# Window attention beside a recurrence: scores in row packs, turned early, with the output divided in the turned layout

## What is computed

```python
def step(yt, wx_t):                      # L2_ffn: t = t + ys
    yt = jax.nn.sigmoid(wx_t + yt @ Vt)
    return (yt, yt)
...
def _window_attn(q, k, v, pos):          # L3_conv: x = x + out, x normed over channels first
    ...
    sim = jnp.einsum('bnhid,bnhjd->bnhij', qh * SCALE, kh) + pos
    attn = jax.nn.softmax(sim, axis=-1)
    out = jnp.einsum('bnhij,bnhjd->bnhid', attn, vh)
    return out.transpose(0, 1, 3, 2, 4).reshape(B, n, m, c)
...
# four quarters of 8 channels, 2 heads of 4: within windows of 8x8 (q1) and 16x16 (q3),
# across windows of 8x8 (q2) and 16x16 (q4)
out = jnp.concatenate([out_1, out_2], axis=-1)
return out @ Wo + bo
```

## Time and profile before

| | |
|---|---|
| median of 3 runs | 1141.13 us (1139.81 to 1141.36) |
| profiled execution, its own time | 1142.24 us |
| its span | 1140.40 us |
| recurrence, first 521 steps | 459.6 to 726.6 |
| the other steps | 726.6 to 1016.8 |
| second half's norm and projections | 1016.8 to 1044.1 |
| the attention's ring and mixing | 1044.1 to 1108.0 |
| experts, output | 1108.0 to the end |

### The profile page before, as it was taken

How to read it: one execution, slowest core, us unless ns; L and a number is a source line. 1 busy time by engine, 2 the same in 40 slices (tenths; PEclk the granted TensorE clock), 3 DMA queues, 4 the chain that set the end, 5 groups by cost and what they waited for, 6 DMA issues and landing times. The chain is left out here.

```text
span 1140.4 us, 12008 instructions
## 1 busy us (share of the span) xinstructions
PE 769.6 (67%) x4425; PEld 447.3 (39%) x4425; DVE 453.1 (40%) x785; ACT 473.4 (42%) x1595; POOL 261.6 (23%) x147
## 2 busy tenths in 40 slices
PE   7917878888768787455555555468985555568986
PEld 3302333333334343333333333346763333335753
DVE  5597999999766546000000000111120000028653
ACT  4446767776436422333333333322223333345542
POOL 3277989898600000300000000000000000002200
PEclk9957999999995687555555555555555555557997
DMA  2020000000000001000000000000000000000000
GB/s 65 2 55 0 1 0 1 1 0 1 1 5 1 1 21 47 24 1 1 0 1 1 1 1 1 1 1 1 1 1 1 0 1 1 1 1 1 1 14 17
DMA packets 9571, 7.70 MB, mean 7 GB/s; under 512 B 7154, under 2 KB 8066, under 8 KB 9224
## 3 DMA queue, kind: packets, MB, share of 16 engines
q1 hardware_dynamic: 9512, 6.93, 2.5%
HBM read 5.09 MB, written 0.26 MB: 5 GB/s over the span
## 5 line engine op out<-in xcount | busy, mean ns | idle before, releaser
L852 PE MATMUL L2p_z<-L2yx,L2v 64*32 64x2 f32 x2048 | 268.6, 199 | 240.3 <-ACT L2yx L862 235.3
L862 ACT ACTIVATE L2yx<-L2p_z 32x2 f32<-32x2 f32 x1024 | 165.0, 161 | 389.3 <-PE L2p_z L852 389.3
L852 PEld LDWEIGHTS L2p_z<-L2yx,L2v 64*32 64x32 f32 x2048 | 180.7, 136 | 337.8 <-ACT L2yx L862 315.5
L750 DVE COPY xn<-L2yx 32x512 f32<-32x512 f32 x2 | 0.8, 417 | 430.9 <-ACT L2yx L862 264.1
L629 POOL TENSOR_TENSOR hc<-hs,cb 128x1024 f32<-128x1024 f32 x64 | 149.4, 2355 | 20.6 <-DVE hs L612 20.5
L1588 POOL COPY xo<-xn 64x256 f32<-64x256 f32 (+1 forms) x6 | 4.0, 692 | 555.4 <-DVE xn L165 555.4
L556 PE MATMUL p_y<-hc,ident 128*128 128x512 f32 x256 | 122.8, 602 | 5.0 <-DVE y_seq L595 2.8
L612 DVE TENSOR_TENSOR_SCAN hs<-d_a,p_bb 128x1024 f32<-128x1024 f32 x48 | 109.8, 2286 | 7.3 <-ACT d_a L579 1.1
L583 ACT ACTIVATE cb<-p_cb 128x1024 f32<-128x1024 f32 x64 | 65.0, 1016 | 7.0 <-PE p_cb L546 6.7
L556 PEld LDWEIGHTS p_y<-hc,ident 128*128 128x128 f32 x256 | 47.7, 191 | 50.0 <-issue 31.5
L579 ACT ACTIVATE d_a<-step,decay 128x1016 f32<-128x1016 f32 x48 | 54.6, 1138 | 23.8 <-DVE hs L612 23.2
(11 more groups left out here) (427 smaller groups left out, 981.1 us busy)
## 6 DMA issues: line engine op xcount, KB each, us to landing
y_seq<-in_pick SPq DMA_DIRECT2D x1, 768.0 KB
b_parts<-part SPq DMA_DIRECT2D x3, 256.0 KB, 3.7
c_parts<-part SPq DMA_DIRECT2D x3, 256.0 KB, 4.5
pos<-in_pos SPq DMA_DIRECT2D x1, 512.0 KB, 3.6
ao<-in_at_o SPq DMA_DIRECT2D x1, 512.0 KB, 4.0
L1w<-in_L_w SPq DMA_DIRECT2D x1, 297.0 KB
L3w<-in_L_w SPq DMA_DIRECT2D x1, 297.0 KB
x_tok<-in_x SPq DMA_DIRECT2D x2, 128.0 KB, 3.0
```

What stands on the lines that cost most here:

```text
L852: pe.matmul(p_z[0:C, t % 2, 0:NB], v[:, 0:C], yx[:, NB * t:NB * (t + 1)], start=True, stop=True).then_inc(s("preact"), 1)
L862: act.activation(yx[0:C, NB * (t + 1):NB * (t + 2)], p_z[0:C, t % 2, 0:NB], ACT.Sigmoid).then_inc(s("state"), 1)
```

## The change

`Front` is made once and works on three *parts*: tiles 0 to 3, tiles 4 to 6, tile 7 (`PARTS`). The first two run beside the recurrence, from steps 517 and 901 on, the last in one block behind it (`rest`), which also holds the whole ring. The norm takes its inverse root on VectorE, by an integer start and three refinements, and has no step on ScalarE. `q` is one tensor; a score reads the 32 rows of its `j`, and the four `j` of a unit stand in four PSUM banks. A unit is now one tile (or two for the 8x8 windows) with all four `j`. For 7 of 12 units scores are made beside the recurrence, the row maximum is subtracted there on VectorE (`shifted`), and the result is turned and copied (`turn_scores`, `copy_turned`); the exponential comes afterwards, on turned scores, over 1024 columns at once, without a sum. Unused columns of the values are ones, so the product with the values gives the sum too, and the output is turned, divided (`divide`) and turned back. Biases and queries carry the other sign, so that VectorE's accumulated minimum is the negated maximum.

The core of the diff:

```diff
-                    HALF, ROOTS = T // 2, T // 2 + 24
-                    first = beside(s2)
+                    HALF, BULK = T // 2, T - 128
+                    front = beside(s2, by_batch)
...
-                            others = first.pe(pe)
+                            others = front.pe(pe)
...
+                                if t == BULK + 5:
+                                    others = itertools.chain(others, front.pe_bulk(pe))
                                 if t > HALF + 4:
                                     next(others, None)
...
-                                if t == ROOTS:
-                                    first.roots(act)
...
-                            add_half(dve, by_batch, 0)
-                            first.dve(dve)
+                            front.add_states(dve, 0)
+                            front.dve(dve)
+                            dve.wait_ge(s("state"), BULK)
+                            front.add_states(dve, 1)
+                            front.dve_bulk(dve)
...
-                            first.pool(pool)
-                    second = beside(s2)
-                    with nc.Block() as block:
...
-                            add_half(dve, by_batch, 1)
-                            second.dve(dve)
...
+                            front.pool(pool)
+                    front.rest(p_z)
...
-        q = sb("q", [128, 2, NB * HEADS, T], stack=st)
...
+        q = sb("q", [128, 2, T], stack=st)
...
-        NU, EARLY = len(units), len(units) // 2
...
+        units = [(2, 0), (2, 1), (2, 2), (2, 3), (0, 0), (0, 2), (0, 4), (0, 6), (2, 4), (2, 5), (2, 6), (2, 7)]
+        NU, FIRST, EARLY = len(units), 6, 7
+        BY_ACT = (8, 10)
...
-                last = dve.tensor_tensor_reduce(scored[:, i % EARLY, c], src[:, c], bias, 1.0, -3e38, ALU.add, ALU.max, mx[:, i, e:e + 1])
...
-                last = act.activation(row, row, ACT.Exp, bias=nmx[:, i, e:e + 1], accum_out=den[:, i, e:e + 1])
...
-                last = dve.tensor_scalar(row, row, rden[:, i, e:e + 1], None, ALU.mult)
...
+            rows = slice(32 * j, 32 * j + 32)
+            if g == 2:
...
+                return pe.matmul(dst[:, 0:KEYS], q[rows, 0, t * 128:(t + 1) * 128], kk[rows, 0, k0:k0 + KEYS], start=True, stop=True)
...
+                ins = dve.tensor_tensor_reduce(scored[:, u % EARLY, j, c], banks[j][:, c], bias, 1.0, 3e38, ALU.add, ALU.min, nmx[:, u, j, n:n + 1])
...
+            dve.tensor_tensor(row, row, least, ALU.subtract).then_inc(sig["at_shifted"], 1)
...
+            PARTS = ((0, 4), (4, 7), (7, 8))
+            ORDER = ((2, 0), (2, 0), (0, 2))
...
+                for _ in range(3):
+                    link(dve.tensor_tensor(step, root, root, ALU.mult))
+                    link(dve.tensor_tensor(step, step, half_var, ALU.mult))
+                    link(dve.scalar_tensor_tensor(root, step, 1.5, root, ALU.add, ALU.mult))
+                dve.tensor_tensor(tok, tok, spread(root), ALU.mult).then_inc(sig["part_scaled"], 1)
...
+            def turn_scores(self, pe, u):
+
+                pe.wait_ge(sig["at_shifted"], u + 1)
+                for n in range(2):
+                    s = 2 * u + n
+                    if s >= 2:
+                        pe.wait_ge(sig["weights_in"], s - 1)
+                    for j in range(NJ):
+                        last = pe.transpose(self.turn_banks[n][:, j * 128:(j + 1) * 128], scored[:, u, j, n * 128:(n + 1) * 128], ident[:])
+                        if j == NJ - 1:
+                            last.then_inc(sig["scores_turned"], 1)
+                        yield
...
+            def score_early(self, pe, u):
+                for n in range(1 if units[u][0] == 2 else 2):
+                    for j in range(NJ):
+                        ins = score(pe, self.early_banks[j], u, j, n)
+                        if units[u][0] == 2 or n == 1:
+                            ins.then_inc(sig["at_scores"], 1)
+                    yield
...
+                for u in range(FIRST):
+                    if u:
+                        pe.wait_ge(sig["at_max"], NJ * u)
+                    yield from self.score_early(pe, u)
+                    if u:
+                        yield from self.turn_scores(pe, u - 1)
+                    for _ in range(4 if u else 9):
...
+            def pe_bulk(self, pe):
+
+                p_q = self.p_q
+                pe.wait_ge(sig["weights_in"], 2 * FIRST)
+                yield from self.turn(pe, 1)
+                for _ in range(12):
+                    yield
+                yield from self.turn_back(pe, 1)
+                for _ in range(4):
+                    yield
+                pe.wait_ge(sig["at_max"], NJ * FIRST)
+                made = 4
+                for k, g in enumerate((2, 0)):
+                    pe.wait_ge(sig["xo_made"], 2 + k + 1)
+                    for m, wgt in enumerate((aq, ak)):
+                        if made >= 6:
+                            pe.wait_ge(sig["qk_read"], made - 1)
+                        self.project(pe, 1, g, wgt, p_q[:, m])
+                        made += 1
+                        for _ in range(3):
+                            yield
+                yield from self.pieces(pe, 0, *self.half_pieces())
+                for _ in range(6):
+                    yield
+                pe.wait_ge(sig["qk_read"], 8)
+                pe.wait_ge(sig["e_read"], 2)
+                yield from self.score_early(pe, FIRST)
+                for _ in range(9):
+                    yield
+                yield from self.turn_scores(pe, FIRST)
+
...
+                dve.wait_ge(sig["e_made"], 2)
+                self.copy_pieces(dve, 0, *self.half_pieces())
+                biased(dve, self.early_banks, FIRST)
+                shifted(dve, FIRST)
+                self.copy_turned(dve, FIRST)
...
+                RING = ["o0", "o1", "b0", "s14", "s15", "b1", "s16", "s17", "o2", "s18", "s19", "b2", "s20", "s21", "s22", "s23",
+                        "out", "o3", "b3"]
...
+                            kt, to = (t // 2 * 2 + n, t) if g == 2 else (t + n, t + n)
+                            for j in range(NJ):
+                                last = pe.matmul(p_o[32 * j:32 * j + 32, to % 4 * 128:(to % 4 + 1) * 128], vv[:, WITHIN[g], kt, j],
+                                                 weights[:, u % EARLY, n, j * 128:(j + 1) * 128], start=(g == 0 or n == 0), stop=(g == 0 or n == 1))
...
+                        def late_scores(u):
+                            for j, n in [(j, n) for j in range(NJ) for n in range(1 if units[u][0] == 2 else 2)]:
+                                if n == 0 and u > EARLY:
+                                    pe.wait_ge(sig["at_max"], NJ * (u - 1) + j + 1)
+                                ins = score(pe, late_banks[j], u, j, n)
+                                if units[u][0] == 2 or n == 1:
+                                    ins.then_inc(sig["at_scores"], 1)
...
+                        keep_streaming(pe, p_o, 2)
+                        for _ in self.turn(pe, 2):
+                            pass
+                        keep_streaming(pe, p_o, 3)
+                        for s in range(6):
+                            values(s)
+                        for _ in self.turn_back(pe, 2):
+                            pass
+                        values(6)
+                        values(7)
+                        for n, (wgt, g) in enumerate(((aq, 0), (ak, 0), (aq, 2), (ak, 2))):
+                            pe.wait_ge(sig["xo_made"], 4 + n // 2 + 1)
+                            self.project(pe, 2, g, wgt, p_q[:, n // 2, n % 2 * 128:(n % 2 + 1) * 128])
+                        for _ in self.pieces(pe, 1, *self.half_pieces()):
+                            pass
+                        for s in range(8, 10):
+                            values(s)
+                        pe.wait_ge(sig["qk_read"], 12)
+                        late_scores(7)
...
+                        values(23)
+                        turn_out()
+                        turn_run(3)
+                        mix_across()
+                        turn_run_back(3)
+                        mix_run(3)
...
+                            link(dve.reciprocal(over, src[:, :, :, HC:HC + 1]))
+                            dve.tensor_tensor(o_norm[:, i % 2, :, 0:16].rearrange("p t (j c) -> p t j c", c=HC), src[:, :, :, 0:HC],
+                                              over.broadcast_to([128, 4, NJ, HC]), ALU.mult).then_inc(read_sem(f"o{i}"), 1)
+
+                        self.add_states(dve, 2)
+                        self.norm(dve, link, 2)
+                        for n, g in enumerate((0, 2)):
+                            dve.wait_ge(sig["qk_made"], 8 + 2 * n + 2)
+                            self.copy_queries(dve, 2, g, p_q[:, n, 0:128])
+                            self.copy_keys(dve, 2, g, p_q[:, n, 128:256])
+                        dve.wait_ge(sig["e_made"], 3)
```

(29 more changed lines are left out.)

900 lines of the change are left out of this document (493 added, 407 removed).

## The result

Over four executions the changed kernel took 1098.77 us in the median (1096.21 to 1100.04), the kernel before 1140.6 on the same chip: a ratio of 0.962 with an interval of 0.960 to 0.964. The forecast was 1102, with a range of 1092 to 1124. The execution that was profiled is the shortest of the four: 1096.21 us, span 1094.3.

What follows compares the result with a forecast made beforehand. Bounds: a 1024-step recurrence chain of matmul and sigmoid (557 us) and 91.2 us of attention behind it. Terms: -3.4 inside, -36 behind (13 + 25 + 8 + 9 = 55), giving 1102 us, range 1092 to 1124.

Steps and rivals of the forecast that it cites:

- the ring: Attention behind the recurrence, passing through TensorE, VectorE and ScalarE in turn; 63.9 us before the change.
- The cost of side work: In the recurrence: step = side work + 0.12 to 0.13, never under 0.5135 us; about 0.39 of every piece free.
- Packs in one matmul's time: In the recurrence: four 32-row score matmuls take the length of one; 5.2 us against 19.7, so -14.5.
- No stall by VectorE, 54 bare steps at the end: In the recurrence: VectorE never stops TensorE; the last 54 steps have no side work.
- 13 us to the values of the last tile: First stretch behind the recurrence: 11 to 15 us, taken as 13, where it took 27.3 before.
- VectorE's list of 25 us with 8 us of waits: Behind the recurrence, up to the last cross output: 25 us of operations, waits 5 for GpSimd and 3 for late handing over.
- The end, 9 us: From the last cross output to the attention's end: 9 us without cover, spreading 4.8 of it.
- Rival 2: Behind the recurrence: TensorE at 1.2 GHz sets the time, nearly 70 us for 55, 1117; chance 0.15 with mixtures.
- Rival 3: In the recurrence: 56 transposes and 10 packs cost 0.77 us each in place of 0.18, above 1143; chance 0.04.
- its 11.6: In the recurrence: the forecast's excess in us for the 56 transposes and 10 packs.
- Rival 4: Behind the recurrence: GpSimd out of the way, clock up early, 8 falls to 2 and 13 to 11, 1094; chance 0.06.
- the forecast's 5 us: Behind the recurrence: 5 us put for VectorE's two-operand operations waiting beside GpSimd's products.

Runs made afterwards that it cites:

- the later edits: Against the changed kernel: third division ahead of second cross scores, 1094.0 us; both cross scores together, 1093.5; that with the ninth unit's subtraction on ScalarE, 1090.8.
- all eight executions: The changed kernel's first four executions and four of the same kernel run again unedited (1096.7 us); median of the eight 1097.3 us.

## Why the prediction was right, step by step

- **The cost of side work** was right for single pieces (projections and packs each within 0.2 us in the sum, small pieces 0.5). The transposes were put at 0.62 a step and took 0.60, 1.0 us less for all 56. The rule behind it was too narrow in one point that no forecast here hung on: the fixed part is paid once in a step, and a second piece costs its columns alone.
- **Packs in one matmul's time**: right, 1.360 against a forecast of 1.32 with some stagger; it was the choice on which most of the stage hung, -13.6 of it net against the forecast's -13.7 (48 old pieces at 19.5 by the trace of before, against 5.9 for all ten packs). By the figure that the Trainium skill gives ("TensorE: Matmul & The Clock Gate", "Measured speedup vs the span model", 3.07 for four row groups) a wide pack was to be 0.26 longer; in this chain it was 0.02.
- **No stall by VectorE, 54 bare steps at the end**: both so; the last piece of side work is the 970th step's.
- **13 us to the values of the last tile**: 10.4 (GpSimd's first product starts at 1021.53, the last sigmoid ends at 1011.13). Up to the normed tile it ran as summed; the four projections and the value pieces then took 3.0 us, and 4.2 was the bottom of my bounds for them together, since value pieces overlap the copies and the clock had come up at 1017.3. This term was the largest miss, under the 11 to 15 given for it.
- **VectorE's list of 25 us with 8 us of waits**: 31.1 in place of 33. The operations alone are 23.4 and the waits 7.8, though differently shared: GpSimd stretched three operations by 3.1 (forecast 5) and VectorE stood 4.7 (forecast 3). That the sum came out at the forecast's 8 is luck, two misses that cancel. The bound named was right, VectorE's list; but two of these waits are one event, since the division that TensorE waited for was queued behind the stretched subtraction.
- **The end, 9 us**: 9.5. The spreading hit a low stretch of the clock.
- **Rival 2** (TensorE at 1.2 GHz sets the time): the clock was at 0.50 for about 20 of the 51 us, yet TensorE was not the bound up to the cross outputs; what is shown of its cost is 1.2 us in the spreading. It became the bound, for 2.1 us, once both cross scores stood together and VectorE was 3.2 us shorter.
- **Rival 3** (slower) needed 0.77 us for each transpose and pack (its 11.6 is 11.8 by the terms ahead of it, which leaves the 0.77); they cost 0.16 in the mean. **Rival 4** (1094) wanted the last tile in 11 us, which came true, and the waits down from 8 to 2, which did not; it took the later edits to get there.

The mechanism held in the parts that a run or a row bears on; how the 23.0 us of the ring divide stays open. Against the forecast's own sum, made for the profiled execution, the changed kernel's profiled execution is 6.6 us shorter: 1.3 from the recurrence, 2.6 from the last tile, 1.9 from the list, less 0.5 at the end, and 1.5 from the parts ahead and behind that the change doesn't touch, less 0.2 of rounding. In the medians 3 of it are left (1098.8 against 1102), with all eight executions 5.

## What to carry to other kernels

Beside a latency chain, price side work by the step: a fixed part once (0.39 us for a transpose here, 0.51 for a matmul of two records, 0.31 for a stream), plus columns. Then cut pieces until they fit under the bare step, as long as steps are left; here 112 halves cost nothing where 56 wholes cost 4.8 us. Put into one step what goes to different row groups, since three more cost 0.02.

When a serial tail is long, look at what it waits for and not at what it computes: three tiles by themselves cost 25 us behind and 8 inside, and in those 25 TensorE and VectorE were busy half of the time. And before moving an operation of two SBUF operands away from GpSimd, see which one takes its place, and whether the engine behind it will be ready for what comes earlier.

## What the runs showed of the hardware

Where an operation of VectorE reads two SBUF operands, it and GpSimd's products exclude each other in these traces; they don't slow each other down. VectorE's subtraction of 128 columns began at 1039.07, GpSimd's product ended at 1041.37, and the subtraction 0.15 us behind that. It goes both ways, as the views of the lines of GpSimd's products show (count, ns min/median/max, first and last start). The long ones in the kernel with both cross scores together:

```profile
L2112 POOL TENSOR_TENSOR pv<-sc,e x2: 2821/3316/3812, 1035.8 to 1038.6; 128x1024 f32<-128x1024 f32 x2
```

and the short ones in the changed kernel:

```profile
L2105 POOL TENSOR_TENSOR prod<-e x8: 292/293/1280, 1025.3 to 1028.1; 128x64 f32<-128x64 f32 x8
```

The long product that had to let VectorE's subtraction of 1024 columns through took 3.81 us and the other 2.82; of the short ones one took 1.28, the one that began while such a subtraction ran (1024.79 to 1026.44), and the others 0.29. Operations with one operand in PSUM (the biasing at 0.42, the division at 0.22) and reductions kept their time beside such products. The Trainium skill says in "SBUF — State Buffer", "Summary: rules for kernel authors", that, when VectorE has two SBUF inputs and GpSimd's operation reads SBUF, the second of the two to issue is blocked until the first is through; these rows agree. Waits for the rest of whole products would have been the better way to work out the forecast's 5 us.

TensorE's granted clock stayed at 0.50 through 14.6 us without a pause, bf16 streams among them, and through 44.2 us without one in the kernel before. It came up 3.6 to 6.8 us after the last sigmoid had started, and after 31.6 us in the kernel with three tiles behind, where TensorE was busy for 14.9 of the first 27.3.
